# Plain attention: where a batch's projections and output chunks stand, and who sends the rows of maxima

## The reference

```python
q = (src @ Wq + bq).reshape(B, T, N_HEAD, HEAD_DIM)
k = (src @ Wk + bk).reshape(B, T, N_HEAD, HEAD_DIM)
v = (src @ Wv + bv).reshape(B, T, N_HEAD, HEAD_DIM)
scores = jnp.einsum('bqhd,bkhd->bhqk', q, k) * scale
probs = jax.nn.softmax(scores, axis=-1)
attn = jnp.einsum('bhqk,bkhd->bqhd', probs, v).reshape(B, T, D_MODEL)
attn = attn @ Wo + bo
x = _layer_norm(src + attn, ln1_g, ln1_b)
...
h = jax.nn.relu(x @ W1[e] + b1[e])
```

## Time and profile before

| | |
|---|---|
| Median of three executions | 2207.73 us (2202.55 to 2209.49) |
| The profiled execution: its time, its span | 2201.22 us, 2199.4 us |
| Plain attention, stretch 0 to 776 us: TensorE busy, mean granted clock | 607 us, 0.83 |
| Busy over the span: TensorE, VectorE, GpSimd, ScalarE | 84%, 59%, 45%, 38% |

### The profile page before, as it was taken

One profiled execution on the slowest core, in us unless ns is written; L12 is line 12 of the kernel. 1 busy time (PEld: TensorE's weight loads), 2 busy tenths in 40 slices (PEclk: granted clock), 3 DMA queues, 4 the chain that ended last, 5 costly groups with the idle time before them and its releaser, 6 DMA issues.

```text
span 2199.4 us, 33971 instructions
## 1 busy us (share of the span) xinstructions
PE 1855.1 (84%) x11505; PEld 1082.6 (49%) x11506; DVE 1291.3 (59%) x2862; ACT 838.3 (38%) x1144; POOL 986.7 (45%) x624
## 2 busy tenths in 40 slices
PE   3877989778888604999759989999998999989998
PEld 1333423324333204999745554655546555564654
DVE  4655656656656342777676556665556655566561
ACT  1534544345454312445314325153341523425242
POOL 3112422332413453444444728357373672737554
PEclk8878968879698856999869999999998999999999
DMA  6235152262232152656330010100101000010000
GB/s 104 46 61 77 27 114 44 37 137 39 42 47 82 46 204 99 233 204 225 129 82 2 1 40 2 29 12 1 39 2 39 1 11 30 1 39 1 10 21 10
DMA packets 72277, 130.31 MB, mean 59 GB/s; under 512 B 11158, under 2 KB 50230, under 8 KB 66236
## 3 DMA queue, kind: packets, MB, share of 16 engines
q1 hardware_dynamic: 69052, 119.89, 21.5%
q0 software_dynamic: 3072, 8.39, 1.2%
HBM read 76.09 MB, written 26.74 MB: 47 GB/s over the span
## 4 chain that ended last, share of the span: by engine, by line
PE 36%; issue 8%; POOL 3%; DVE 3%; ACT 1%; POOLq 0%; DMA 0%; SPq 0%; DVEq 0%; ACTq 0%
PE a_psS L703 10%; PE a_psO L717 9%; PE a_psO L740 6%; PE a_psM L677 4%; PE a_psS L665 4%; PE a_psS L649 2%; POOL a_k_tok L350 1%; PE a_psS L730 1%; ACT a_probs L468 1%; POOL a_oT L373 1%; POOL a_q_tok L350 1%; DVE a_junk L534 1%; DVE a_alibi L611 0%; DVE a_rden L548 0%; DVE a_turned L542 0%
## 5 line engine op out<-in xcount | busy, mean ns | idle before, releaser
L385 POOL TENSOR_TENSOR a_probs<-a_probs 128x1024 f32<-128x1024 f32 x144 | 340.7, 2391 | 346.6 <-PE a_psO L717 346.6
L534 DVE CUSTOM_DVE_ANT_0 a_junk<-a_psM,a_alibi 128x512 bf16<-128x512 f32 x512 | 333.7, 689 | 245.4 <-PE a_psM L677 244.2
L1272 DVE TENSOR_REDUCE f_n_tok<-f_psR 128x1 f32<-128x512 f32 x512 | 324.2, 682 | 243.1 <-PE f_psR L1408 242.2
L468 ACT ACTIVATE a_probs<-a_psS 128x1024 f32<-128x1024 f32 x256 | 249.7, 1024 | 311.4 <-PE a_psS L703 311.3
L1216 ACT ACTIVATE f_probs<-f_psS 128x1024 f32<-128x1024 f32 x256 | 248.0, 1023 | 271.6 <-PE f_psS L1427 270.7
L717 PE MATMUL a_psO<-a_probs,a_v 128*32 128x512 f32 x2048 | 244.0, 597 | 0.0
L1408 PE MATMUL f_psR<-f_kP,f_qP 48*128 48x512 f32 x512 | 189.0, 567 | 49.5 <-DVE f_n_tok L1272 35.8
L1408 PEld LDWEIGHTS f_psR<-f_kP,f_qP 48*128 48x128 f32 x512 | 74.1, 215 | 267.1 <-issue 132.8
L1427 PE MATMUL f_psS<-f_qP,f_kP 64*128 64x512 f32 x512 | 130.6, 493 | 70.1 <-DMA f_qP<-f_n_row 69.2
L1440 PE MATMUL f_psO<-f_probs,f_v 128*32 128x512 f32 x1024 | 170.4, 744 | 0.7 <-ACT f_probs L1216 0.6
L677 PE MATMUL a_psM<-a_kH,a_qH 64*128 64x512 f32 x512 | 128.2, 493 | 35.6 <-DVE a_n_tok L534 27.8
(11 more groups left out here) (190 smaller groups left out, 3566.6 us busy)
## 6 DMA issues: line engine op xcount, KB each, us to landing
w_w_high<-w_parts SPq DMA_DIRECT2D x19, 1024.0 KB
w_w_low<-w_parts SPq DMA_DIRECT2D x19, 1024.0 KB
f_kP<-f_high SPq DMA_DIRECT2D x64, 128.0 KB, 4.5
f_qP<-f_high SPq DMA_DIRECT2D x64, 128.0 KB, 6.4
e_xs<-sorted_x SPq DMA_DIRECT2D x19, 256.0 KB, 2.7
sorted_z<-e_z SPq DMA_DIRECT2D x19, 256.0 KB, 2.2
sorted_x<-f_zeros SPq DMA_DIRECT2D x7, 640.0 KB, 8.9
f_xn<-in_L_attn_x SPq DMA_DIRECT2D x8, 512.0 KB, 3.9
```

Of the source, the lines that this page charges most:

```text
L385: nc.gpsimd.tensor_tensor(slots, slots, probs[:, first - GRP:first - GRP + 2, :], ALU.add).then_inc(added.sem, 1)
L468: nc.scalar.activation(probs[:, slots, :], psS[:, 2 * p:2 * p + 2, :], ACT.Exp).then_inc(exp_done.sem, 1)
L534: nc.vector.tensor_tensor_reduce(out=junk[:, a, :], in0=psM[:, a, :], in1=alibi[:, h, :], scale=1.0, scalar=-3.0e38, op0=ALU.add, op1=ALU.max,
L1272: nc.vector.tensor_reduce(n_tok[:, c, column:column + 1], psR[:, ring_bank("max", u), :], AX.X, ALU.max, negate=True).then_inc(max_done.se ...
```

## The change

- **Extras.** The four `out` chunks of the batch before leave (0,2) and (0,3), two in each, for (2,0), (2,1), (2,3) and (3,0), one in each. `v`, `proj` and `maxima` keep their periods. VectorE's statistics of the rows (`norm1`) go from (2,3) to (3,1).
- **oT** gets two places, used by batches in turn.
- **Rows of maxima.** ScalarE issues the two DMAs itself, right behind its cast, after waiting for the cast to be done. SyncE's queue has none of them any more: it issues both groups of moves, then W1's store and load, the clearing of rows, and the next load of x.
- **W1** goes through in eight pieces of 128x1024, one in each batch, in place of four of 128x2048 in every second.
- **GpSimd's order** within a batch is changed (below), and its filling of `kP` and `qP` at the start waits until VectorE has normalised the first rows.

The core of the diff:

```diff
-    EXTRAS = {(0, 1): [("v", 1)], (0, 2): [("out", 0), ("out", 1)], (0, 3): [("out", 2), ("out", 3)],
-              (1, 0): [("proj", 0)], (1, 1): [("proj", 1)], (1, 2): [("maxima", 2), ("proj", 2)],
-              (1, 3): [("proj", 3)], (2, 2): [("maxima", 3)], (3, 2): [("maxima", 0)], (3, 3): [("v", 0)]}
-    EXTRAS[0, 2] = [("maxima", 1)] + EXTRAS[0, 2]
+    EXTRAS = {(0, 1): [("v", 1)], (0, 2): [("maxima", 1)], (1, 0): [("proj", 0)], (1, 1): [("proj", 1)],
+              (1, 2): [("maxima", 2), ("proj", 2)], (1, 3): [("proj", 3)], (2, 0): [("out", 0)], (2, 1): [("out", 1)],
+              (2, 2): [("maxima", 3)], (2, 3): [("out", 2)], (3, 0): [("out", 3)], (3, 2): [("maxima", 0)],
+              (3, 3): [("v", 0)]}
...
-        oT = sb("oT", [P, QUADS, S])
+        oT = sb("oT", [P, 2, QUADS, S])
...
             norm0.raise_variance(pool, 0)
+            pool.wait_ge(xn_done.sem, xn_done.at(0, TT - 1))
             nc.gpsimd.memset(kP[:, :, :].bitcast(F32), 1.0).then_inc(zeroed, 1)
...
                 nc.scalar.copy(n_row[:, n % 2, :],
                                psR[0:4, ring_bank("maxima", n), :]).then_inc(n_row_done.sem, 1)
+                act.wait_ge(n_row_done.sem, n_row_done.at(b, n))
+                place = place_of(b, QP * n)
+                for a in range(2):
+                    row = FB * a + NEG
+                    act.dma_start(qP[row:row + 1, place:place + QP, :].bitcast(F32),
+                                  n_row[QP * a:QP * (a + 1), n % 2, :].bitcast(F32)).then_inc(n_moved.sem, 16)
...
-                        if quad == 1 and before:
-                            act.wait_ge(out_ps.sem, out_ps.at(b - 1, TT - 1))
+                        if quad == 1 and b > 1:
+                            act.wait_ge(out_ps.sem, out_ps.at(b - 2, TT - 1))
...
-                    if (quad, j) == (2, 3) and before:
+                    if (quad, j) == (3, 1) and before:
                         dve.wait_ge(r1_done.sem, r1_done.at(b - 1, TT - 1))
                         norm1.statistics(dve, b - 1, r1)
```

More of the change, by code:

```diff
@@ L998, in move_sides, with load_w1, store_w1 @@
                                          part[FB * a:FB * (a + 1), n, :].bitcast(F32)).then_inc(moved[g].sem, 16)
-            def move_maxima(b, quad):
-                sp.wait_ge(n_row_done.sem, n_row_done.at(b, quad))
-                first_place = place_of(b, QP * quad)
-                for a in range(2):
-                    row = FB * a + NEG
-                    sp.dma_start(qP[row:row + 1, first_place:first_place + QP, :].bitcast(F32),
-                                 n_row[QP * a:QP * (a + 1), quad % 2, :].bitcast(F32)).then_inc(n_moved.sem, 16)
-            def load_w1(e):
-                sp.dma_start(w1_raw[:, :, :], w["W1"][e].rearrange("(c p) n -> p c n", p=P)).then_inc(w1_in, 16)
-            def store_w1(e):
-                sp.wait_ge(w1_rest, e + 1)
+            def load_w1(n):
+                sp.dma_start(w1_raw[:, :], w["W1"][n // KC].rearrange("(c p) n -> c p n", p=P)[n % KC]).then_inc(w1_in, 16)
+            def store_w1(n):
+                sp.wait_ge(w1_rest, n + 1)
                 for part, tile in enumerate((w1_high, w1_low)):
-                    sp.dma_start(w1_parts[e, part], tile[:, :, :].rearrange("p c n -> p (c n)").bitcast(F32))\
-                        .then_inc(w1_stored, 16)
+                    sp.dma_start(w1_parts[n // KC, part].rearrange("p (c n) -> c p n", c=KC)[n % KC],
+                                 tile[:, :].bitcast(F32)).then_inc(w1_stored, 16)
             def load_rows(b):
@@ L1105, in normalize @@
                 pool.wait_ge(rsum_done.sem, rsum_done.at(b, quad))
-                nc.gpsimd.tensor_tensor(oT[:, quad, :], oT[:, quad, :], rsum[:, :], ALU.mult)\
+                nc.gpsimd.tensor_tensor(oT[:, b % 2, quad, :], oT[:, b % 2, quad, :], rsum[:, :], ALU.mult)\
                     .then_inc(norm_done.sem, 1)
@@ L1146, in batch @@
                     normalize(b - 1, QUADS - 1)
+                if more:
+                    low_part(b + 1, 0)
+                    low_part(b + 1, 1)
+                normalize(b, 0)
+                if more:
+                    low_part(b + 1, 2)
+                    low_part(b + 1, 3)
+                normalize(b, 1)
                 add_bias_to_rows(b, not before)
@@ L1149, in batch @@
                     keep_rows(b + 1)
-                    low_part(b + 1, 0)
-                normalize(b, 0)
-                if more:
-                    low_part(b + 1, 1)
-                normalize(b, 1)
-                if more:
-                    low_part(b + 1, 2)
-                    low_part(b + 1, 3)
                 if before:
@@ L1205, in take_maxima @@
                                psR[0:4, ring_bank("maxima", n), :]).then_inc(n_row_done.sem, 1)
+                act.wait_ge(n_row_done.sem, n_row_done.at(b, n))
[4 more added lines that the diff above has]
+                                  n_row[QP * a:QP * (a + 1), n % 2, :].bitcast(F32)).then_inc(n_moved.sem, 16)
             def take_output(b, quad):
                 act.wait_ge(pv_done.sem, pv_done.at(b, TT * quad + TT - 1))
-                nc.scalar.copy(oT[:, quad, :], psO[:, :]).then_inc(o_taken.sem, 1)
+                nc.scalar.copy(oT[:, b % 2, quad, :], psO[:, :]).then_inc(o_taken.sem, 1)
             def exponentials(b, r, p):
@@ L1276, in invert_sums @@
                 dve.wait_ge(o_taken.sem, o_taken.at(b, quad))
-                nc.vector.transpose(turned[:, :], oT[:, quad, :]).then_inc(turned_done.sem, 1)
+                nc.vector.transpose(turned[:, :], oT[:, b % 2, quad, :]).then_inc(turned_done.sem, 1)
                 dve.wait_ge(turned_done.sem, turned_done.at(b, quad))
@@ L1379, in project_output @@
                 for quad in range(QUADS):
-                    last = nc.tensor.matmul(bank[:, 0:D], oT[:, quad, t * P:(t + 1) * P], wo[:, quad, :],
+                    last = nc.tensor.matmul(bank[:, 0:D], oT[:, b % 2, quad, t * P:(t + 1) * P], wo[:, quad, :],
                                             start=(quad == 0), stop=(quad == QUADS - 1))
```

37 lines of the change are left out of this document (14 added, 23 removed).

## The result

The changed kernel takes 2091.5 us in the median of four runs (2078.2 to 2097.6), the kernel before 2206.8 (2202.6 to 2209.5). The ratio is 0.947, with a 95% interval from 0.942 to 0.952. The forecast was 2092. The profiled execution of the changed kernel took 2089.4 us, its span is 2087.3 and its mean granted clock 0.931, against 0.898 before.

A forecast was written before the change was run, and what follows sets the result against it. TensorE's waits for the late row of maxima, and slow-clock matmuls behind them, bound the kernel. 6 x 16.7 + 15 - 1 + 7 - 5 = 116 us off 2201.2 gives 2085, as median 2092; range 2066 to 2142.

The forecast's parts named there:

- the start: First rows: VectorE's normalisation no longer runs beside GpSimd's fills, so everything behind shifts earlier; gain 7 us, between 4 and 8.
- The last batch and the end: Batch 7 pays for ScalarE, loss 1 us; later statistics of batch 6 delay the last multiplication, loss 5, between 3 and 6.
- The landing: Rows of maxima for quads 2 and 3, sent from ScalarE's queue: land in 1.2 to 3 us, so no wait.
- rival A: Before (2,0) and (3,0): the row still waits behind the moves; 2112 us, or 2167 if the clock falls; chance 0.23.
- ScalarE's issue: Behind its casts, ScalarE issuing two DMAs delays the exponentials: 3 x 1.0 = 3.0 us a batch lost, range 1.5 to 4.5.
- B: Behind ScalarE's casts: its issue costs twice SyncE's price, 1.3 us more at three places in seven batches; 2119 us, chance 0.07.
- The six periods: (2,0) to (3,1): 25.7 us with four output chunks, full clock and no waits, against 38.0; gain 12.3 us a batch.
- (0,2) and (0,3): These two periods lose two output chunks each: gain 7.4 us a batch.
- W1 in eight pieces: W1's transfers, one piece in each batch: same bytes and nearly the same work, off the path; costs nothing.
- GpSimd and the load of x: Later load of x and GpSimd's later chain in each batch: both hidden, the load with 7 us to spare.
- C: Next batch's x or GpSimd's results come late: 4 us too late costs 28 us, giving 2120; chance 0.05.
- D: Quads 2 and 3: the clock stays low, 7 us lost a batch; slower, 2240 us; chance 0.04.

## Why the prediction was right, and where its steps were not

Against the profiled executions the sum was 116 us; TensorE's last products of the stage moved by 117.5. By parts: the start gave 63.55 - 57.01 = 6.5 (forecast 7). Batches 0 to 6 gave 620.8 - 505.4 = 115.4 (forecast 15 + 6 x 16.7 = 115.2). The last batch and the end lost 73.7 - 69.3 = 4.4 (forecast 1 + 5). The span gained 5.4 us less than the stage: its last part, from the first store of the result to the last, took 907.4 us before and 913.0 after. The rows of these stores, before and after (min, median and max ns of one, first and last start in us):

```profile
L313 SPq DMA_DIRECT2D out<-a_acc x8: 389/395/406, 1288.7 to 2196.1; - x8
```

```profile
L313 SPq DMA_DIRECT2D out<-a_acc x8: 389/396/406, 1170.9 to 2083.9; - x8
```

With the same instructions that part took between 906.0 and 919.6 us in the other executions, so this is scatter.

That the total fits so well hides two wrong terms that cancelled.

*The landing.* I took 1.2 to 3 us, because a second queue need not stand behind the first one's packets. It was 5.6 and 4.7 us. This is the step that failed, and rival A's premise is what held: for quad 2 beside the moves, for quad 3 beside W1 and the clearing, for with these held it is 1.1 to 2.0 in batches 1 to 6. The Trainium skill's rule ("DMA: Bandwidth & Descriptors", section "Issuing engines are not separate DMA queues"), that another engine saves only the time of issuing, agrees with these landings. What the send saved is the place in SyncE's order. Of the 4.0 us between cast and end of issue, 2.7 were spent behind the last moves and 1.3 on the row's own issue; from ScalarE they are 0.03 and 1.17, so 2.8 us are saved, and the wait before (2,0) went from 3.27 to 0.57. A's price was too high, not its mechanism: it gave 0.8 and 2.5 us of waits, found were 0.57 and 0.92 in batch 1, at most 1.4 anywhere, with the full clock right behind them in batches 1 to 6 and 0.60 in batch 0. The second was smaller than A's 2.5 because issue and landing took 5.8 us, not 7.0, and (2,3) without its wait some 4.7, not 4.5. A's clock was also added up wrongly: half of 13 us is 6.5 a batch and not 8 to 9, so A came to 2151 and not 2167. And the lower end of the forecast's range does not follow from its two terms: 1.5 us for ScalarE and 4.3 for a chunk period in six batches give 2078, not 2066.

*ScalarE's issue.* I took 1.0 us at each of three places and it was about a third of one: at (2,2) by the idle times above, at (0,2) by the run with SyncE's sends, which passes (0,3) in 3.7 us where the changed kernel takes 4.0. The idle time of ScalarE absorbed the rest. The doubled issue shows where that ends: the next 1.26 us cost 44 us. So B's price for them, 27, was too low, as it left out the row that leaves later.

*What took the place of the 3.0 us.* The six periods came to 26.85 us for 25.7, all of it in (2,3), 5.7 us for 4.5: by the traffic of W1 and the clearing, since it is 4.6 where they are held. (0,2) and (0,3) gave 7.0 for 7.4. And (3,2) takes 4.8 us where the kernel before took 3.8: by the statistics at (3,1), since it is 3.85 where they are spread. Together 2.6. I had W1 in eight pieces at nothing, as "the same bytes and nearly the same work, off the path", and the statistics inside (3,1) alone. Both were costed on their own engine and in their own period, not in what they do to a transfer in flight or to the period that comes next. The first could have mattered: with the chunks in their old place the same traffic costs 38 us.

*The cause named.* I gave the cure of both waits to the send. It is enough for most of it, but before (3,0) GpSimd's order would have done it without; I had read that order for its own chain and not for the moves that wait for it.

*The rest.* GpSimd and the load of x were hidden, C did not happen. VectorE's statistics of the new rows wait for x at the start only. The clock of the six periods is 1.00 in batch 1 and 0.99 on average over batches 2 to 5, D did not happen. Batch 0 took 71.0 where 69.5 was forecast, with a stretch at 0.60 in it. The start was within half a us, by the cause named. At the end, the last multiplication was late by what was worked out from the earlier trace rows.
